# Two expert tables in place of one, a single result row per token, and a re-ordered chunk loop in an RWKV + mixture-of-experts kernel

## The chip, the cores and the metric

The kernel runs on one core of a Trainium2 chip. The metric is the device time of one execution in microseconds (us). Engines: PE is TensorE, ACT is ScalarE, DVE is VectorE, POOL is GpSimd, and SP issues plain DMAs. POOL issues the indirect DMAs, which scatter 128 rows at a time to row numbers held in SBUF.

## The reference, cut to what matters

The first half (time mixing, a log-space recurrence over 2048 tokens of each of 8 sequences) is untouched but for the order of a few steps. The second half is the mixture of experts: each of N = 16384 tokens goes through a shared expert and through its two best of 8 routed ones, and the two kinds of results are added before the last layer norm.

```python
x = x + layernorm(attn(layernorm(x), ...))              # x is (8, 2048, 256)
# ffn on xf = layernorm(x), n = 16384 tokens, d = 256, E = 8, K = 2
probs = softmax(xf @ router_w)
topw, topi = top_k(probs, 2)
combine[n, topi] += topw
h = silu(einsum('nd,edf->nef', xf, w1)); ye = einsum('nef,efd->ned', h, w2)
routed = einsum('ne,ned->nd', combine, ye)
shared = sigmoid(xf @ shared_gate_w) * (silu(gate) * up @ shared_down)
x = x + layernorm(routed + shared)
```

## The kernel before, in words

There are four stages, one after the other.

**The chunk loop** takes the tokens in NCH = 32 chunks of TC = 512. It is a software pipeline: in loop turn i, PE projects chunk i-1 (`proj`), and works on the output product, the router and the shared expert of chunks i-3 to i-5; every engine has its own such list of steps, written out by hand, and the lists are held together by semaphores alone. Each engine does its list in order. Per chunk, DVE picks the two experts (`route`), turns the ranks that PE sums up (`ranks`, bf16 products of the choice masks) into row numbers `ixs` (`place`) and writes the weights behind the token's normed row `h2n` (`weights`). POOL then scatters the row twice, once per choice (`scatter(m, 0)` and `scatter(m, 1)`, four indirect DMAs of 128 rows each), into `d_xd`, which has one region per expert. `h2n` is one buffer, so ACT writes the next chunk's rows (`h2_normed`) only after all eight scatters of the chunk before have landed; POOL computes the scale for it (`scale_h2`) behind those scatters in its own queue. The shared expert's result `ysh`, halved by `weights`, is written by SP to both rows that a token has in `d_y` (lines 402 to 405). During turns 17 to 32, every other turn, ACT and DVE split one expert's weights into a high and a low part (`experts_high`, `experts_low`), one 128x1024 operation each.

**The transition.** After the last chunk, DVE makes the table of blocks (`counted` and the steps behind it: for each block of BLK = 256 rows its expert and its start row), SP writes zero rows behind each expert's last row (`tails`, 8 regions and one more, each with a register load from `tail`), and loads the first blocks.

**The block loop** runs over NB = 2N/BLK + 7 = 135 blocks of 256 rows of one expert. For each, SP loads the rows (`load_block`, four buffers), PE transposes them (`block_in`, 4 instructions), multiplies by w1 (`block_hidden`, 12) and, two blocks later, by w2 (`block_out`, 12); ACT and DVE split each operand into high and low parts; DVE weighs the result into one of six buffers `yb` (`y_out`), and POOL adds it to `d_y` by two indirect DMAs with `compute_op=add` (lines 544 to 548). DVE's `ends` waits for the scatter of eight blocks ago. PE waits at three places for signals that PE itself gives: `s_yp` in `block_in`, `s_Tx` in `block_hidden`, `s_hid` in `block_out`.

**The final stage** goes over the 32 chunks again: SP loads the two rows per token from `d_y` (`y0C`, `y1C`) and x1 (`load_rest`; 12 chunks of it are already loaded in the block loop), DVE adds the two (`total`) and takes the statistics (`stats`), POOL makes the scale (`norm_scale`), ACT applies it, DVE adds x1 (`final`), SP writes the output.

## Time and profile before

| what | value |
|---|---|
| time, median of 3 runs | 1822.88 us (1819.39 to 1824.19) |
| the profiled execution | 1824.77 us |
| span from its first to its last instruction | 1822.6 us |
| PE busy | 1518.0 us (83% of the span) |
| DVE busy | 1466.1 us (80%) |
| ACT busy | 1395.4 us (77%) |
| POOL busy | 1076.9 us (59%) |
| mean granted TensorE clock | 0.928 |

The busy times are means over four stages with different limits, so they are read by stretch: to about 1030 us the chunk loop, to 1134.8 us the transition, to 1658.3 us the block loop and its last scatters, then the final stage. The span and the profiled execution differ by 2.2 us, which lies outside of the first and the last instruction.

### The profile page before, as it was taken

The page shows a single profiled execution, that of the slowest core. Times are in us where ns is not written, and L with a number is a line of the kernel's source. Part 1 is how long each engine was busy: PE and PEld are TensorE (multiplying, and loading weights), DVE is VectorE, ACT ScalarE, POOL GpSimd, SP SyncE. Part 2 cuts the span into 40 slices and gives each one's busy share as a digit, 9 for nine tenths or more (in the row PEclk, how much of TensorE's full clock was granted, in tenths as well). Part 3 has the DMA queues.
Part 4 walks back from the last instruction along what each step waited for, and adds up shares of the span by engine and source line. Part 5 has one row for each costly group of instructions (what it writes and reads, how often), then busy time and mean ns, then how long its engine had stood idle before and what let it go on. Part 6 is the DMA issues. An engine that isn't in the chain of part 4 may idle for free.

```text
span 1822.6 us, 34848 instructions
## 1 busy us (share of the span) xinstructions
PE 1518.0 (83%) x9764; PEld 1346.6 (74%) x9764; DVE 1466.1 (80%) x3533; ACT 1395.4 (77%) x2577; POOL 1076.9 (59%) x985
## 2 busy tenths in 40 slices
PE   4899999999999999999999935999999999980000
PEld 3688888888888888888888835999888888870000
DVE  4799989999998998989999844887777776764888
ACT  3799999999999999999999853776666666652434
POOL 1245546455563654646555351788888888886556
PEclk8999999999999999999999966999999999995555
DMA  6123434343333433334333234998888888877997
GB/s 202 47 84 118 136 115 139 118 144 105 118 119 106 142 106 107 126 99 142 106 116 108 75 128 158 249 181 144 144 145 146 143 146 143 146 114 232 417 417 299
DMA packets 184043, 274.67 MB, mean 151 GB/s; under 512 B 17712, under 2 KB 139568, under 8 KB 183856
## 3 DMA queue, kind: packets, MB, share of 16 engines
q1 hardware_dynamic: 132688, 201.37, 32.8%
q0 software_dynamic: 51168, 71.07, 22.4%
q8 instruction: 84, 1.38, 0.3%
q14 instruction: 103, 0.84, 0.2%
HBM read 127.53 MB, written 144.85 MB: 149 GB/s over the span
## 4 chain that ended last, share of the span: by engine, by line
PE 51%; issue 12%; POOL 10%; DVE 9%; DMA 9%; ACT 2%; DVEq 2%; SPq 1%; POOLq 0%; ACTq 0%
PE PS L1283 39%; POOL d_y L547 7%; PE PS L1275 3%; PE PS L1459 2%; PE PS L1477 2%; POOL d_xd L522 2%; DMA d_y<-nx,ixb 2%; DMA d_y<-x,ixb 2%; PE PS L1346 2%; PE PS L1344 2%; DMA d_y<-xin,ixb 2%; DVE bst L877 1%; DMA rkl<-d_y 1%; DMA al<-d_y 1%; DMA shl<-d_y 1%
## 5 line engine op out<-in xcount | busy, mean ns | idle before, releaser
L522 POOL DMA_INDIRECT d_xd<-h2n,ixs x256 | 319.4, 1248 | 271.6 <-DVE h2n L1056 190.3
L1283 PE MATMUL PS<-hTh,wqh 128*128 128x512 f32 x768 | 307.4, 400 | 16.8 <-ACT kk L581 11.5
L1283 PE MATMUL PS<-hTh,wql 128*128 128x512 f32 x768 | 306.9, 400 | 0.0
L1283 PE MATMUL PS<-hTl,wqh 128*128 128x512 f32 x768 | 306.5, 399 | 0.0
L1283 PEld LDWEIGHTS PS<-hTh,wqh 128*128 128x128 f32 x768 | 146.8, 191 | 53.0 <-ACT kk L581 12.4
L547 POOL DMA_INDIRECT d_y<-xin,ixb x90 | 143.4, 1593 | 52.5 <-DVE xin L1229 28.5
L1283 PEld LDWEIGHTS PS<-hTh,wql 128*128 128x128 f32 x768 | 146.3, 191 | 34.6
L1283 PEld LDWEIGHTS PS<-hTl,wqh 128*128 128x128 f32 x768 | 146.9, 191 | 33.3
L547 POOL DMA_INDIRECT d_y<-nx,ixb x90 | 142.5, 1584 | 27.4 <-issue 21.9
L547 POOL DMA_INDIRECT d_y<-x,ixb x90 | 142.2, 1580 | 27.4 <-issue 19.8
L482 POOL TENSOR_SCALAR var<-mv 128x4 f32<-128x4 f32 x64 | 64.4, 1006 | 154.4 <-DVE mv L882 154.2
L502 POOL TENSOR_SCALAR var<-sq 128x4 f32<-128x4 f32 x32 | 8.7, 272 | 172.4 <-ACT sqo L672 172.4
L1283 PE MATMUL PS<-h2h,wgh 128*128 128x512 f32 x256 | 106.6, 416 | 0.0
L1477 PE MATMUL PS<-weh,h2h 128*128 x360 | 106.1, 295 | 0.0
L1283 PE MATMUL PS<-h2l,wgh 128*128 128x512 f32 x256 | 101.4, 396 | 0.0
L1477 PE MATMUL PS<-weh,h2l 128*128 x360 | 101.2, 281 | 0.0
L1477 PE MATMUL PS<-wel,h2h 128*128 x360 | 101.2, 281 | 0.0
L1283 PE MATMUL PS<-h2h,wgl 128*128 128x512 f32 x256 | 100.9, 394 | 0.0
L1459 PE MATMUL PS<-rkh 128*128 128x256 f32 x268 | 80.4, 300 | 15.9 <-DVE rkl L1239 12.7
L1459 PE MATMUL PS<-hTh,shh 128*128 128x256 f32 x272 | 82.4, 303 | 11.8 <-DVE shl L1239 5.8
L485 POOL TENSOR_TENSOR rstd<-var,mhalf 128x4 f32<-128x4 f32 x64 | 87.0, 1359 | 5.3
L826 ACT ACTIVATE al<-PS 128x512 f32<-128x512 f32 x90 | 53.9, 599 | 44.2 <-PE PS L1459 37.7
(301 smaller groups left out, 5631.8 us busy)
## 6 DMA issues: line engine op xcount, KB each, us to landing
d_y<-ysh SPq DMA_DIRECT2D x64, 512.0 KB
xin<-in_L_attn_x SPq DMA_DIRECT2D x32, 512.0 KB, 3.9
x<-in_L_attn_x SPq DMA_DIRECT2D x32, 512.0 KB, 3.9
d_x<-x SPq DMA_DIRECT2D x32, 512.0 KB
kk<-d_xd SPq DMA_DIRECT2D x34, 272.0 KB
vv<-d_xd SPq DMA_DIRECT2D x34, 272.0 KB
tr<-d_xd SPq DMA_DIRECT2D x34, 272.0 KB
dl<-d_xd SPq DMA_DIRECT2D x33, 272.0 KB
```

What stands on the lines that cost most here:

```text
L482: g.tensor_scalar(var[:, w, :], mvw[:, :, 1], EPS, None, ALU.add).then_inc(s_va[w], 1)
L485: g.tensor_tensor(rstd[:, w, :], var[:, w, :], mhalf[:, :], ALU.pow).then_inc(s_rs[w], 1)
L522: g.indirect_dma_start(d_xd, bass.IndirectOffsetOnAxis(ap=ixs[:, k:k + 1], axis=0), h2n[:, j, :], None).then_inc(s_sct, 16)
L547: g.indirect_dma_start(d_y, bass.IndirectOffsetOnAxis(ap=ixb[:, w % 8, j:j + 1], axis=0), yb[w % NYB][:, j, :], None, compute_op=ALU.add). ...
L826: A.activation(sil[u % 3], hidB[u % 3][:, :], ACT.Silu).then_inc(s_sil, 1)
L877: V.bn_stats(bst[:, k, j, :], tile(j)).then_inc(s_bst[w], 1)
L1275: ins = nc.tensor.transpose(bank[a][:, j * P:(j + 1) * P], src[:, j, a * P:(a + 1) * P], ident[:, :])
L1283: ins = mm_(out_ap, l, r, start=(k == 0), stop=(k == len(todo) - 1))
L1344: mm_(both, h2h[:, a, at], rwp[:, a, :], start=(a == 0), stop=False)
L1346: ins = mm_(both[:, 0:RW], h2l[:, a, at], rwp[:, a, 0:RW], start=False, stop=(a == H - 1))
L1459: ins = mm_(hidB[u % 3][:, f * D:(f + 1) * D], l, r, start=(k == 0), stop=(k == len(todo) - 1))
L1477: ins = mm_(outB[w % 3][:, j * D:(j + 1) * D], l, r, start=(k == 0), stop=(k == len(todo) - 1))
```

## The change

- **Two tables.** The blocks of first choices and those of second choices are kept apart: `d_xd` becomes two tensors, `tb`, `pos`, `cnt`, `tail`, `tabo/x/e/p` get a leading index of 2, and there are NB1 = 64 + 7 = 71 blocks per choice, NB = 142 in all.
- **One row per token.** `d_y` has N rows. The shared result is scattered by POOL (`shared_scatter`, four indirect DMAs per chunk) into `d_xs`, in the order of the first choices. In the first 71 blocks SP loads those rows into `yb` (`load_shared`), DVE adds the routed result to them, and POOL writes them by indirect DMAs without `compute_op`. The other 71 blocks are added with `compute_op=add` as before; POOL starts them when all of the first 71 have landed. The final stage loads one row per token; `total` is gone.
- **Tails.** SP writes 16 of them before the first block (8 of `d_xd[0]`, 8 of `d_xs`), plus three at fixed rows, and the 8 of the second table (`tail_2`) behind the loads of blocks 1 to 8.
- **Order.** The experts' weights are split in the turns NCH+2 and NCH+3 of the loop. `ranks` of the last two chunks is put between the two halves of the gate product. K's, V's, up's and the ranks' PSUM banks are dealt out anew, with another order of `up` and `proj(0)` on PE. `own_exp` moves from the start of a turn to the end of the one before, `weighed` behind `shared`. POOL does `scale_in` last in a turn, with `shared_scatter` behind it.
- **PE's waits for its own signals** in the three block functions are gone.

```diff
-    NB = 2 * N // BLK + E - 1
-    NF = 2 * N // BLK
+    NF = N // BLK
+    NB1 = NF + E - 1
+    NB = 2 * NB1
...
-        pV = [PS[1], PS[5]]
+        pV = [PS[1], PS[0]]
...
-        pU = [PS[4], PS[3]]
+        pU = [PS[0], PS[3]]
...
-        pRT, pRK = PS[0], PS[0]
+        pRT, pRK = PS[0], PS[4]
...
+                for s in range(2):
+                    sp.dma_start(d_xd[s][E * CAP:E * CAP + BLK, :].rearrange("(p j) d -> p j d", p=P), zt
+                                 ).then_inc(s_tail, 16)
+                sp.dma_start(d_xs[E * CAP:E * CAP + BLK, :].rearrange("(p j) d -> p j d", p=P), zt[:, :, 0:D]
+                             ).then_inc(s_tail, 16)
                 sp.wait_ge(s_tab, 1)
                 for e in range(E):
...
+                for e in range(E):
+                    r = sp.value_load(tail[0:1, 0, e:e + 1], min_val=0, max_val=E * CAP - BLK)
+                    sp.dma_start(d_xs[bass.ds(r, BLK), :].rearrange("(p j) d -> p j d", p=P), zt[:, :, 0:D]).then_inc(s_tail, 16)
...
-                if i - 6 == NCH - 1:
-                    tails()
-                if on(i - 6):
-                    sp.wait_ge(s_ys, n(i - 6, NT, NT))
-                    for s in range(2):
-                        sp.dma_start(ys_a[s, i - 6], ysh[:, :, :]).then_inc(s_st2, 16)
...
+            tails()
...
+            sp.wait_ge(s_scy, 16 * NT * NCH)
...
+            def load_shared(b):
+                if b >= NYB:
+                    sp.wait_ge(s_yo[b % NYB], 32 * (b // NYB))
+                r = sp.value_load(tabx[0:1, 0, b:b + 1], min_val=0, max_val=E * CAP)
+                sp.dma_start(yb[b % NYB], d_xs[bass.ds(r, BLK), :].rearrange("(p j) d -> p j d", p=P)
+                             ).then_inc(s_yl[b % NYB], 16)
...
             for b in range(NB):
+                if b == NB1:
+                    sp.wait_ge(s_tail2, 16 * E)
                 load_block(b)
+                if 1 <= b <= E:
+                    tail_2(b - 1)
...
+                if 0 <= b - 2 < NB1:
+                    load_shared(b - 2)
...
+            def shared_scatter(m):
+                pool.wait_ge(s_pl, n(m, NPL, L_IX))
+                for j in range(NT):
+                    pool.wait_ge(s_ys, n(m, NT, j + 1))
+                    g.indirect_dma_start(d_xs, bass.IndirectOffsetOnAxis(ap=ixs[:, m % 2, j:j + 1], axis=0),
+                                         ysh[:, j, :], None).then_inc(s_scy, 16)
...
-            for i in range(NCH + 4):
+            for i in range(NCH + 6):
...
+                if on(i - 4):
+                    scale_o(i - 4)
+                if i - 6 == NCH - 2:
+                    shared_scatter(i - 6)
+                if on(i - 5):
+                    scatter(i - 5, 0)
+                    scatter(i - 5, 1)
+                if on(i - 4):
+                    scale_h2(i - 4)
                 if 0 < i < NCH:
                     scale_in(i)
...
+                if on(i - 6) and i - 6 != NCH - 2:
+                    shared_scatter(i - 6)
...
+                    if w == NB1:
+
+                        for i in range(NYB):
+                            pool.wait_ge(s_yo[i], 32 * ((NB1 - i + NYB - 1) // NYB))
...
+                if i == NCH + 2:
+                    experts_high(EORDER[0:4])
                 if on(i - 4):
                     h2_normed(i - 4)
...
-                if 17 <= i < 17 + 2 * E and i % 2:
-                    experts_high([(i - 17) // 2])
                 if on(i - 3):
                     squares_o(i - 3)
+                if i == NCH + 2:
+                    experts_high(EORDER[4:7])
...
+                if m >= 2:
+
+                    dve.wait_ge(s_sct, 16 * 2 * NT * (m - 1))
+                    dve.wait_ge(s_scy, 16 * NT * (m - 1))
+                V.tensor_copy(ixs[:, m % 2, :], posa[:, :]).then_inc(s_pl, 1)
...
+                if i == NCH + 3:
+                    experts_low(EORDER[3:E])
...
+                    if w < NB1:
+                        V.scalar_tensor_tensor(out=t, in0=part, scalar=cwb[:, w % 8, j:j + 1], in1=t, op0=ALU.mult,
+                                               op1=ALU.add).then_inc(s_y, 1)
...
-            def total(c):
...
+                if NCH - 2 <= i - 4 < NCH:
+
+                    free((i - 4, s_h2l, 2, 2), (i - 2, s_tr, 2, 2), (i - 5, s_pl, NPL, L_TB))
+                    ranks(i - 4)
...
-                    if a and t >= 4:
-                        pe.wait_ge(s_yp, t - 3)
...
-                        if f == 0 and k == 3 and u + 1 < NB:
-
-                            pe.wait_ge(s_Tx, u + 2)
...
-                        if j == 0 and k == 3:
-                            pe.wait_ge(s_hid, min(w + 3, NB))
```

## Rows read from the trace of the kernel before

**Rows 1.** Busy time by stretch: from:to, length, engines, PEclk, DMA share, GB/s
```profile
200.00:400.00 200.00, 200.00 (x1175) 172.58 (x1174) 182.22 (x451) 192.09 (x369) 107.15 (x105) 1.00 0.38 124
1140.00:1658.00 518.00, 467.20 (x3741) 445.40 (x3740) 366.90 (x936) 322.29 (x533) 428.13 (x270) 0.98 0.87 152
1700.00:1750.00 50.00, 0.00 (x0) 0.00 (x0) 39.67 (x97) 20.24 (x40) 27.83 (x40) 0.50 1.03 416
```

**Rows 2.** The same view, a loop turn without and one with an expert's weights
```profile
512.50:544.40 31.90, 31.90 (x189) 27.48 (x188) 28.42 (x67) 30.62 (x59) 16.86 (x16) 1.00 0.34 118
544.40:577.25 32.85, 32.25 (x189) 27.56 (x188) 30.87 (x75) 31.45 (x62) 16.08 (x20) 1.00 0.36 115
```

**Rows 3.** Costliest groups, then POOL's timeline in one turn: start, us, engine, operation
```profile
L522 POOL DMA_INDIRECT d_xd<-h2n,ixs x256 | 319.4, 1248 | 271.6 <-DVE h2n L1056 190.3
...
436.57 1.94 POOL L522 DMA_INDIRECT d_xd<-h2n,ixs  x1 [0.30 <-issue]
...
441.35 0.96 POOL L522 DMA_INDIRECT d_xd<-h2n,ixs  x1 [0.30 <-issue]
...
450.62 0.26 POOL L487 TENSOR_TENSOR nb<-nmx,rstd 128x4 f32<-128x4 f32 x1
```

**Rows 4.** Timeline of DVE in the turn before: row numbers, then weights
```profile
428.40 0.17 DVE L1033 CAST ixs<-posa 128x8 uint32<-128x8 f32 x1
...
429.35 0.19 DVE L1047 TENSOR_REDUCE ssum<-pw 128x4 f32<-128x32 f32 x1 [0.37 <-ACT pw L721]
```

**Rows 5.** Timeline of ACT: an expert's high part, and the last chunks' normed rows
```profile
712.58 1.04 ACT L574 CAST weh<-wel 128x1024 fp32r<-128x1024 f32 x1
...
1060.17 1.04 ACT L739 CAST rkh<-ee 128x1024 fp32r<-128x1024 f32 x1 [2.91 <-DVE ee L1068]
1061.38 2.08 ACT L657 ACTIVATE h2n<-x,nb,rstd 128x256 f32<-128x256 f32 x4 [0.16 <-POOL nb L514]
```

**Rows 6.** Timeline of DVE, POOL and SP in the transition
```profile
1106.36 0.19 DVE L1020 TENSOR_TENSOR pos<-PS,tb 128x32 f32<-128x32 f32 x1 [3.90 <-PE PS L1366]
...
1109.39 1.07 POOL L522 DMA_INDIRECT d_xd<-h2n,ixs  x1 [18.49 <-DVE h2n L1056]
...
1119.51 1.07 POOL L522 DMA_INDIRECT d_xd<-h2n,ixs  x1 [0.30 <-issue]
...
1114.31 10.15 SPq L375 DMA_DIRECT2D d_xd<-vv  x8
...
1128.27 0.37 SPq L422 DMA_DIRECT2D kk<-d_xd  x1
```

**Rows 7.** Chain that ended last, its ends of the block stage: start, us, what
```profile
1134.81 2.91 PE PS L1459 x12
...
1628.18 1.62 PE PS L1459 x12
...
1654.51 3.75 DMA d_y<-x,ixb
```

**Rows 8.** Groups of 1200 to 1600 us (busy, mean ns), then timelines of POOL and PE
```profile
L547 POOL DMA_INDIRECT d_y<-x,ixb x72 | 114.1, 1585 | 21.9 <-issue 15.8 <-DVE x L1229 3.1 <-DVE ixb L1221 2.7
...
1146.01 1.70 POOL L547 DMA_INDIRECT d_y<-xin,ixb  x1 [25.43 <-DVE xin L1229]
...
1184.63 0.66 PE L1437 MATMUL PS<-ident,kk 128*128 128x128 f32 x4
...
1188.02 0.66 PE L1437 MATMUL PS<-ident,vv 128*128 128x128 f32 x4
```

**Rows 9.** Timeline of DVE and POOL in the final stage
```profile
1673.71 1.22 DVE L1254 TENSOR_TENSOR ysh<-h2h,rkl 128x1024 f32<-128x1024 f32 x1
...
1677.88 1.22 DVE L1254 TENSOR_TENSOR h2n<-h2l,shh 128x1024 f32<-128x1024 f32 x1
...
1741.36 1.31 POOL L482 TENSOR_SCALAR var<-mv 128x4 f32<-128x4 f32 x1 [2.02 <-DVE mv L882]
...
1744.18 0.21 POOL L487 TENSOR_TENSOR nb<-nmn,rstd 128x4 f32<-128x4 f32 x1
```

More of the change, by code:

```diff
@@ L52, in rwkv_moe @@
     out_c = out.rearrange("b (c p j) d -> (b c) p (j d)", j=NT, p=P)
-    d_xd = nc.dram_tensor("d_xd", [E * CAP + BLK, XW], F32).ap()
-    NSINK = E + NB - NF + 1
-    d_y = nc.dram_tensor("d_y", [2 * N + 1 + NSINK * BLK, D], F32).ap()
-    ys_a = d_y[1:2 * N + 1, :].rearrange("(s c j p) d -> s c p j d", s=2, j=NT, p=P)
+    d_xd = [nc.dram_tensor(f"d_xd{s}", [E * CAP + BLK, XW], F32).ap() for s in range(2)]
+    d_xs = nc.dram_tensor("d_xs", [E * CAP + BLK, D], F32).ap()
+    NSINK = E + NB1 - NF + 1
+    d_y = nc.dram_tensor("d_y", [N + 1 + NSINK * BLK, D], F32).ap()
     with ExitStack() as ctx:
@@ L275, in rwkv_moe @@
         s_yo = [sem(f"s_yo{i}") for i in range(6)]
+        s_yl = [sem(f"s_yl{i}") for i in range(6)]
         s_Tx = sem("s_Tx")
@@ L286, in rwkv_moe @@
         s_y = sem("s_y")
-        s_cx = [sem(f"s_cx{i}") for i in range(12)]
-        s_cy2 = [sem(f"s_cy2{i}") for i in range(6)]
-        s_sum = sem("s_sum")
+        s_cx = [sem(f"s_cx{i}") for i in range(14)]
         s_nrm = sem("s_nrm")
@@ L297, in rwkv_moe @@
         NRO = 7
[L299 to L300 removed]
+        L_POS, L_TB, L_PM, L_POSA, L_IX, L_DST = range(1, 7)
+        NPL = 6
         W_SUM, W_CWT, W_SG, W_CW = range(2, 6)
@@ L386, in _ @@
             sp.dma_start(x1[:, :, :], x_v[0]).then_inc(s_xr, 16)
-            for i in range(NCH + 6):
+            for i in range(NCH + 4):
                 if i % 2 == 0 and i // 2 < E:
@@ L545, in _ @@
                 pool.wait_ge(s_y, 2 * (w + 1))
-                for j in range(2):
-                    g.indirect_dma_start(d_y, bass.IndirectOffsetOnAxis(ap=ixb[:, w % 8, j:j + 1], axis=0),
-                                         yb[w % NYB][:, j, :], None, compute_op=ALU.add).then_inc(s_yo[w % NYB], 16)
+                if w < NB1:
+                    for j in range(2):
+                        g.indirect_dma_start(d_y, bass.IndirectOffsetOnAxis(ap=ixb[:, w % 8, j:j + 1], axis=0),
+                                             yb[w % NYB][:, j, :], None).then_inc(s_yo[w % NYB], 16)
+                else:
+                    if w == NB1:
+                        for i in range(NYB):
+                            pool.wait_ge(s_yo[i], 32 * ((NB1 - i + NYB - 1) // NYB))
+                    for j in range(2):
+                        g.indirect_dma_start(d_y, bass.IndirectOffsetOnAxis(ap=ixb[:, w % 8, j:j + 1], axis=0),
+                                             yb[w % NYB][:, j, :], None, compute_op=ALU.add).then_inc(s_yo[w % NYB], 16)
             for c in range(NCH):
@@ L1152, in _ @@
                 if on(i - 3):
+                    weighed(i - 3)
                     sums(i - 3)
@@ L1202, in _ @@
             step(11)
+            both = [P, 2, NBP]
+            V.tensor_tensor(tbf[:, 1, :, :], tbf[:, 1, :, :], iot2[:, :].unsqueeze(1).to_broadcast(both), ALU.add
+                            ).then_inc(s_tb, 1)
+            step(12)
             V.tensor_scalar(iot2[:, :], iot2[:, :], -(NF - 1.0) * BLK, None, ALU.add).then_inc(s_tb, 1)
-            step(12)
-            V.scalar_tensor_tensor(out=tabo[:, :], in0=tbf[:, 0, :], scalar=E - 0.5, in1=iot2[:, :], op0=ALU.is_ge,
-                                   op1=ALU.mult).then_inc(s_tab, 1)
```

252 lines of the change are left out of this document (126 added, 126 removed).

## The prediction

> **What bounds the kernel now.** I read busy time by stretch first. In the chunk loop PE is busy 200.00 of 200 us at full clock, with ACT at 192 and DVE at 182; in the block stage PE is at 90% and POOL at 83%, and the DMA share is 0.87; in the final stage the DMA share is 1.03 at 416 GB/s and no engine is near full [rows 1]. The timelines then tell what the block stage hangs on. One `compute_op=add` scatter holds POOL for 1.585 us, plus 0.30 us between two, so a block's two take 3.77 us [rows 8], while PE, where nothing holds it, starts a block every 3.39 us (transposes at 1184.63 and 1188.02) [rows 8]. And PE's last product starts at 1628.18 while POOL's last scatter starts at 1654.51, 26 us later [rows 7]: POOL bounds the block stage. So there are four limits: PE, then a latency chain in the transition, then POOL, then DMA bytes.
>
> **Chunk loop.** A turn takes 31.90 us without an expert's weights and 32.85 with them [rows 2]; ACT has only 1.3 us to spare in the first kind, and the cast takes 1.04 of it [rows 5]. Eight such turns become plain: 8 x 0.95 = **-8 us**. PE's own work per turn is unchanged (`ranks` is wider, still 11 tiny products), and the new order and banks put no wait where an operand is late in the trace, so I cost them at nothing; so also `own_exp`, `weighed` and the one operation fewer in `place`. That cover is PE's: DVE and ACT have a turn's rest of 3.5 and 1.3 us [rows 2].
>
> What is added is `shared_scatter`, four indirect DMAs on POOL per chunk. The kind's mean is 1.248 us, the least 0.96, and 1.94 where DVE's scans run beside it [rows 3]; with 0.30 between, four take 6.2 us, or 5.0 to 9.0. They stand behind `scale_in`, which ends at 450.88 [rows 3], so they end at 457.1, and land 2.2 us later (the last block scatter took 3.75 us from its start to its landing, 1.55 of it on POOL [rows 7, 8]): 459.3. Who waits? `place` of the next chunk must not write `ixs` before: that cast is due at 428.40 + 31.9 = 460.3, and behind it on DVE stand `weights` and the residual, for which POOL's next scatters and PE wait [rows 4]. The wait is covered by 1.0 us, and `weights` itself has 0.37 us more, since it waits for ACT [rows 4]. I take nothing, and keep 0 to 1.8 us per turn for the range: 1.8 is what four scatters of 1.94 give (450.9 + 9.0 + 2.2 = 462.1 against 460.3).
>
> How long a scatter takes beside DVE decides this. The row shows 1.94 us against 0.96 for the same instruction [rows 3]. The Trainium skill (GPSIMD Engine Reference, Key points) says that GpSimd shares its SBUF interfaces with VectorE and contends with instructions "in a 2-port perf mode or with two SBUF inputs"; by that rule the new scatters, beside DVE's subtractions from PSUM with one SBUF input, would mostly run in 0.96, and if all four were blocked the sum would be that of the slower rival below.
>
> **Transition**, two chains. (a) ACT casts four experts before `h2_normed` of chunk 30. In the trace that starts at 1061.38, right behind the cast that ends at 1061.21 [rows 5], so four casts of some 0.97 us each come on the path: +3.7. Three more stand before the exponentials of chunk 30, for which `weights` had 0.85 us of cover in `place`: about +1.8, since the earlier `ranks` gains nothing there. So chunk 31's routing comes 5.5 us later. The five low parts on DVE and ACT's last cast fall in DVE's idle time after 1081. For chunk 31 `ranks` comes 3.7 us earlier (DVE waited 3.90 us for it [rows 6]), so the table is only 2 us later. (b) POOL's last eight scatters took from 1109.39 to 1120.58 [rows 6]. Now chunk 30's shared scatters stand before them and wait for its down product (+5.5, to about 1120.6), then eight (11.2) and four (5.1): 1137, and 2.2 to land, 1139.1, before SP may load block 0. SP's chain is shorter: the tails cost 1.27 us each (10.15 for 8) [rows 6], 16 of them 20.3, from about 1110: 1130.4, landed 2.5 later. So the first load moves from 1128.27 [rows 6] to about 1139.5, 11 later. I take **+10**, 4 to 16: the lower end has POOL's part overlap better, the upper has contended scatters and longer table steps.
>
> **Block stage**, from PE's first product at 1134.81 to the last landing at 1658.26: 523.5 us [rows 7]. After: the first scatter comes 11.2 us in [rows 7, 8]. A first-choice block takes POOL only 2 x (0.96 + 0.30) = 2.5 us, if a plain block scatter costs what a plain row scatter does [rows 3], so PE bounds those: 3.39 less what the dropped waits cost, under 0.1, for they stand behind three products or transposes already issued: 3.35. 70 x 3.35 = 234.5. Then 2.5 for the last, 2.2 to land, as POOL waits for all; PE runs on meanwhile. Then 142 x (1.585 + 0.30) = 267.7, and 1.9 for the landing: 11.2 + 234.5 + 2.5 + 2.2 + 267.7 + 1.9 = 520.0, **-3**. The seven blocks more thus eat what the cheap scatters give. Range -9 (1.85 per scatter as in its uncontended form) to +11 (blocks at 3.55: loads of shared rows and x1 together). DVE adds from SBUF in `y_out` instead of only weighing, beside PE; its share is 71% [rows 1].
>
> **Final stage**, 1822.6 - 1658.3 = 164.3 us. Bytes before: 33.6 MB of `d_y`, 10.5 of x1 (20 chunks), 16.8 out: 60.8 MB, at 416 GB/s 146 us, so 18 lie at the ends. After: 16.8 + 9.4 + 16.8 = 43.0 MB, 103 us; with the same ends 121. What is late next: DVE's chunk takes 1677.88 - 1673.71 = 4.17 us where data is there; without `total` (1.22 and a gap of 0.04) 2.91, 93 us for 32. POOL's takes 1741.36 to 1744.39, 3.03, and some 0.15 between [rows 9]: 102, about as much as the bytes. So I take 121, **-43**, with 112 to 132 (POOL at 3.6 per chunk if it contends).
>
> The Trainium skill (DMA: Bandwidth & Descriptors, Where 436 GB/s comes from) gives about 358 GB/s as the HBM limit of a core; by that figure the stage would take 120 + 18 = 138 and the gain be 26. The trace shows 416 over 50 us [rows 1], so the measurement decides.
>
> **Sum**, against the profiled execution's span: 1822.6 - 8 + 10 - 3 - 43 = 1778.6. That execution took 1824.77, 1.9 above the median, so the same 44 off the median gives 1822.88 - 44 = **1779**.
>
> **Rivals.** *A, plain scatters are no cheaper in the block loop.* Then POOL bounds both halves: 142 x 1.885 = 267.7 instead of 234.5 (and 1.2 more for the last), +34 minus the little that PE's slack gives: 1811. For it: the two kinds differ in source buffer and row length, not only in the addition. Against: 1.55 never goes below in 270 scatters, 0.96 is the usual of 256.
> *B, the place where the shared scatters stand is too tight.* 0.5 to 1.2 us per turn, in 31 turns: +15 to +37, 1794 to 1816. For it: cover of 1.0 us only. Against: the mean scatter fits.
> *C, slower than before.* The same wait, when every one of the four shared scatters runs at the doubled 1.94 us: 1.8 us per turn x 31 = 56, 1835. It decides from 1.45 us per turn (44/31), that is from a shared scatter of 1.84 us on average. Against it: 0.96 is usual where DVE does not scan, and after 451 it does not.
> *D, the edges are kinder:* transition +4, block stage -9, final stage -52 (bytes alone, shorter ends): 1822.88 - 65 = 1758 at the far end.
>
> **How the numbers follow.** Forecast 0.70 (1766 to 1794); A 0.08; B 0.12; C 0.03; D beyond 1765 0.07. The range leaves out C, most of A and of D: 1763 to 1802. A measurement of this kernel tells 0.3%, some 5.5 us, from no change. Faster by more: everything but C and the end of B, 0.95; within: 0.02; slower: 0.03.
>
> **What would show it.** Right: turns 17 to 32 of 31.9 us; POOL's scatters of 0.96 us and PE's blocks of 3.35 in the first half of the block loop, 3.77 in the second, with a POOL backlog only in the second; a final stage of 121 us with DMA still near 1.0. Wrong: a wait of DVE before `ixs` in every turn (B, C); 1.55 us for plain block scatters (A); a final stage paced by POOL at 3.6 us per chunk; first load later than 1145, above all if POOL's scatters were not last there but SP's tails.

## The result, and the profile after

The changed kernel took **1779.08 us** (median of 4, 1778.62 to 1782.03) against 1822.88 before: ratio 0.9766, interval 0.9749 to 0.9783. Its profiled execution has a span of 1776.9 us, 45.7 under before's 1822.6. That is the predicted time. It is not the whole result: run again later, the same kernel took 1816.29 at the same mean granted clock (0.936, against 0.937; run `c1_after_again` below), and most of the experiments went into why.

First the stages of the profiled execution, each end read from a timeline (PE's last product of chunk 31's projections, PE's first product of the blocks, the last landing, the end):

```
stage                        before   after    change   predicted
projections of chunk 31 end  1030.70  1019.11   -11.6      -8
transition                    104.11   113.45    +9.3     +10
block stage                    523.5    522.0    -1.4      -3
final stage                    164.3    122.3   -42.0     -43
```

Busy time by stretch, kernel after, to be laid beside [rows 1]; the block stage is split where the adding scatters begin:

```profile
200.00:400.00 200.00, 200.00 (x1183) 172.93 (x1183) 182.23 (x432) 192.55 (x367) 132.75 (x130) 1.00 0.33 111
1140.00:1380.00 240.00, 235.52 (x2007) 233.86 (x2006) 203.09 (x503) 172.46 (x288) 156.00 (x141) 1.00 0.86 274
1385.00:1654.00 269.00, 226.20 (x1882) 219.95 (x1880) 183.15 (x469) 160.03 (x264) 224.46 (x142) 0.96 0.85 136
1633.00:1654.00 21.00, 0.00 (x0) 0.00 (x0) 0.53 (x2) 0.00 (x0) 16.48 (x11) 0.51 0.63 74
1700.00:1750.00 50.00, 0.00 (x0) 0.00 (x0) 39.85 (x125) 28.23 (x55) 33.81 (x55) 0.50 1.00 393
```

In the loop PE is still full and POOL has gone from 107 to 133 us in 200. In the first half of the blocks PE is at 98% and POOL at 65%; in the second POOL, not PE, sets the pace. The final stage still has the DMA engines full.

The `PEclk` column is 1.00 in the first two rows. The 0.96 of the third is its end alone: PE's last product ends at 1630.3, the granted clock goes to half at 1633.3 and stays there (fourth row, 0.51), and from 1385 to 1633 it is 1.00. So the clock costs the blocks nothing here.

The loop's new scatters, in POOL's timeline, and behind them DVE's cast that must wait for them (compare [rows 3] and [rows 4]):

```profile
480.56 1.08 POOL L553 DMA_INDIRECT d_xs<-ysh,ixs  x1 [0.47 <-issue]
...
484.66 0.96 POOL L553 DMA_INDIRECT d_xs<-ysh,ixs  x1 [0.30 <-issue]
...
489.71 0.17 DVE L1086 CAST ixs<-posa 128x8 uint32<-128x8 f32 x1
```

```profile
DVE ixs L1086 <- DMA d_xs<-ysh,ixs: 2.5, 6, 0.6
```

```profile
L553 POOL DMA_INDIRECT d_xs<-ysh,ixs x76: 956/1023/1227, 321.6 to 898.4; - x76
...
DMA to landing us min/median/max: 2.4/3.6/5.3
```

The second fence is DVE's list of waits in 300 to 900 us (total, times, longest): the shared scatters made the cast wait six times, 2.5 us in all. The third has their durations in the same stretch (ns, shortest, median, longest) and the time from the start of one to its landing. Their place is wide enough, but only just: in the 25 turns from 160 to 940 us the last rows of a chunk land 2.4 to 4.4 us after POOL's scatter ends (median 3.0), and the cast follows that landing by 1.0 us in the median, in seven turns at once. No turn is longer for it.

The transition, timelines of ACT, POOL and SP, then SP's waits in 1095 to 1135 us (compare [rows 5] and [rows 6]):

```profile
1046.94 3.88 ACT L618 CAST weh<-wel 128x1024 fp32r<-128x1024 f32 x4
1050.72 2.07 ACT L701 ACTIVATE h2n<-x,nb,rstd 128x256 f32<-128x256 f32 x4
...
1107.12 1.79 POOL L546 DMA_INDIRECT d_xd<-h2n,ixs  x1 [0.31 <-issue]
...
1118.97 0.96 POOL L553 DMA_INDIRECT d_xs<-ysh,ixs  x1 [0.30 <-issue]
...
1122.77 0.96 POOL L553 DMA_INDIRECT d_xs<-ysh,ixs  x1 [0.31 <-issue]
...
1107.67 10.78 SPq L385 DMA_DIRECT2D d_xs<-ee  x8
1126.11 0.38 SPq L432 DMA_DIRECT2D kk<-d_xd  x1
```

```profile
SPq L422 <- DMA d_xs<-ysh,ixs: 6.7, 1, 6.7
```

Four casts stand before `h2_normed`; POOL's row of twelve scatters ends at 1123.73, after SP's tails at 1118.45; and SP then waits for the last shared rows before it loads a block that doesn't need them.

The blocks, timelines of PE and POOL and the end of the chain (compare [rows 7] and [rows 8]):

```profile
1246.07 0.60 PE L1499 MATMUL PS<-ident,tr 128*128 128x128 f32 x4
1249.31 0.60 PE L1499 MATMUL PS<-ident,dl 128*128 128x128 f32 x4
...
1380.21 1.26 POOL L583 DMA_INDIRECT d_y<-nx,ixb  x1 [0.30 <-issue]
1385.08 1.61 POOL L591 DMA_INDIRECT d_y<-x,ixb  x1 [3.60 <-DVE xin L1295]
...
1650.98 3.58 DMA d_y<-xin,ixb
```

```profile
L583 POOL DMA_INDIRECT d_y<-nx,ixb x48 | 54.0, 1125 | 26.7 <-DVE nx L1292 16.1 <-issue 10.6
...
L591 POOL DMA_INDIRECT d_y<-xin,ixb x48 | 75.9, 1582 | 14.6 <-issue 11.9 <-DVE ixb L1279 1.8 <-DVE xin L1295 0.6
```

A first-choice block starts every 3.26 us on average (3.24 to 3.28 by turns) instead of 3.40; a plain scatter holds POOL for 1.1 us, an adding one for 1.58; between the halves POOL stands 3.60 us; from 1385.08 to 1650.98 lie 141 scatters of 1.886 each.

### The profile page after: what moved, and what is told of

It is laid out like the page before. It is cut to its first block, busy times and chain, and to the rows that moved or that the text cites. A ratio compares the mean times of both kernels' runs of the same rounds, so it can differ in the third digit from the quotient of the medians.

```text
span 1776.9 us, 36129 instructions
## 1 busy us (share of the span) xinstructions
PE 1512.4 (85%) x9960; PEld 1359.6 (77%) x9960; DVE 1451.5 (82%) x3518; ACT 1408.8 (79%) x2605; POOL 1149.0 (65%) x1127
## 3 DMA queue, kind: packets, MB, share of 16 engines
q8 instruction: 86, 1.41, 0.3%
## 4 chain that ended last, share of the span: by engine, by line
PE 65%; POOL 8%; DMA 7%; issue 7%; DVE 4%; ACT 3%; SPq 2%; DVEq 1%; POOLq 0%; ACTq 0%
PE PS L1341 46%; PE PS L1518 6%; PE PS L1534 5%; POOL d_y L591 5%; PE PS L1333 3%; PE PS L1499 2%; DMA d_y<-x,ixb 2%; PE PS L1404 2%; DMA d_y<-nx,ixb 2%; PE PS L1402 1%; POOL d_xd L546 1%; DMA d_y<-xin,ixb 1%; DVE bst L925 1%; DMA dl<-d_y 1%; POOL var L506 1%
## 5 line engine op out<-in xcount | busy, mean ns | idle before, releaser
L546 POOL DMA_INDIRECT d_xd<-h2n,ixs x256 | 317.8, 1241 | 234.5 <-DVE h2n L1108 164.1
L1341 PE MATMUL PS<-hTh,wqh 128*128 128x512 f32 x768 | 306.1, 399 | 16.3 <-ACT kk L625 10.6
L553 POOL DMA_INDIRECT d_xs<-ysh,ixs x128 | 134.8, 1053 | 58.8 <-issue 45.3
L1341 PEld LDWEIGHTS PS<-hTl,wqh 128*128 128x128 f32 x768 | 146.1, 190 | 33.1
L1534 PE MATMUL PS<-weh,h2l 128*128 x380 | 106.2, 279 | 0.0
L1534 PE MATMUL PS<-wel,h2h 128*128 x380 | 106.1, 279 | 0.0
L1518 PE MATMUL PS<-rkh 128*128 128x256 f32 x284 | 86.4, 304 | 12.1 <-DVE rkl L1304 10.6
L509 POOL TENSOR_TENSOR rstd<-var,mhalf 128x4 f32<-128x4 f32 x64 | 92.9, 1451 | 5.3
L1518 PE MATMUL PS<-hTh,shh 128*128 128x256 f32 x284 | 86.5, 305 | 7.8 <-DVE shl L1304 7.8
L865 ACT CAST hTh<-PS 128x512 fp32r<-128x512 f32 x71 | 41.7, 587 | 60.2 <-PE PS L1499 60.2
L591 POOL DMA_INDIRECT d_y<-x,ixb x48 | 75.5, 1573 | 17.9 <-issue 10.7
L591 POOL DMA_INDIRECT d_y<-xin,ixb x48 | 75.9, 1582 | 14.6 <-issue 11.9
L583 POOL DMA_INDIRECT d_y<-xin,ixb x48 | 52.5, 1093 | 48.1 <-DVE xin L1292 40.2
```

The source lines that it names most:

```text
L509: g.tensor_tensor(rstd[:, w, :], var[:, w, :], mhalf[:, :], ALU.pow).then_inc(s_rs[w], 1)
L546: g.indirect_dma_start(d_xd[s], bass.IndirectOffsetOnAxis(ap=ixs[:, m % 2, k:k + 1], axis=0), h2n[:, j, :], None).then_inc(s_sct, 16)
L553: g.indirect_dma_start(d_xs, bass.IndirectOffsetOnAxis(ap=ixs[:, m % 2, j:j + 1], axis=0), ysh[:, j, :], None).then_inc(s_scy, 16)
L583: g.indirect_dma_start(d_y, bass.IndirectOffsetOnAxis(ap=ixb[:, w % 8, j:j + 1], axis=0), yb[w % NYB][:, j, :], None).then_inc(s_yo[w % NY ...
L591: g.indirect_dma_start(d_y, bass.IndirectOffsetOnAxis(ap=ixb[:, w % 8, j:j + 1], axis=0), yb[w % NYB][:, j, :], None, compute_op=ALU.add). ...
L865: copy(xTh[t % 2], PS[t % 2][:, :]).then_inc(s_xh, 1)
```

## The experiments

Twelve kernels ran, in four series; each was timed beside the kernel before, whose medians were 1821.24, 1822.45, 1821.41 and 1822.10 us. The spans and stretches below are of each kernel's profiled execution.

### PE's waits for its own signals

`e1_before_no_own_waits` (series 1), before without them:

```diff
-                    if a and t >= 4:
-                        pe.wait_ge(s_yp, t - 3)
...
-                            pe.wait_ge(s_Tx, u + 2)
...
-                            pe.wait_ge(s_hid, min(w + 3, NB))
```

> The kernel before with PE's three waits for its own signals taken out of the blocks, nothing else. My theory: all 135 blocks of before end at the pace of POOL's adding scatters (2 x 1.885 us a block against some 3.4 us of PE), so the time stays, 0 us, within 1; PE's busy time in a block may fall by 0.13 us without anybody asking for it. Rival: the waits hold up the chain of every block, and the time falls by 135 x 0.13 = 18 us.

Measured: 1822.65 us, ratio 1.0005 (0.9989 to 1.0022). The theory holds. While POOL has not yet fallen behind, PE runs full in both kernels, and the waits can be read off: same stretch 1145 to 1210 us, first the kernel before, then this one:

```profile
1145.00:1210.00 65.00, 65.00 (x536) 63.27 (x535) 55.58 (x135) 46.27 (x78) 53.93 (x34) 1.00 1.00 247
```

```profile
1145.00:1210.00 65.00, 65.00 (x560) 65.00 (x559) 53.62 (x134) 48.13 (x80) 54.73 (x34) 1.00 1.00 250
```

560 products instead of 536 in the same 65 us, or 3.26 us a block instead of 3.40: **0.14 us a block**. The loads of weights (PEld) are at 63.27 with the waits and at 65.00 without: the little gap is there. POOL's adds take it all back.

`e2_after_own_waits` (series 1), after with them:

```diff
+                    if a and t >= 4:
+                        pe.wait_ge(s_yp, t - 3)
...
+                            pe.wait_ge(s_Tx, u + 2)
...
+                            pe.wait_ge(s_hid, min(w + 3, NB))
```

> The kernel after with PE's three waits for its own signals put back in both halves of the blocks. My theory: the first 71 blocks are PE-bound now, their pace goes from 3.27 us back to 3.40 us, and the time rises by 71 x 0.13 = 9 us (against after's 1779.1: 1788); the second half, bound by the adding scatters at 2 x 1.886 us a block, doesn't change. Rival, the value of the prediction: the waits cost under 0.04 us a block, the faster pace has another reason (XW rows, the table loads, the shorter scatter), and the time rises by 3 us or less.

Measured: 1831.63 us, 1.0053 (1.0036 to 1.0070): 53 above after's first measurement, where the theory said 9. In the second half PE's blocks take 3.40 us while it catches up, as expected (1441.92 to 1516.90, 22 of them). In the first half they take 4.1. PE's waits in 1150 to 1430 us, and one of them with DVE's and POOL's timeline:

```profile
PE PS L1501 <- PE PS L1540: 28.8, 41, 0.9
```

```profile
1214.25 0.96 POOL L583 DMA_INDIRECT d_y<-nx,ixb  x1 [0.30 <-issue]
...
1215.84 0.88 DVE L1292 SCALAR_TENSOR_TENSOR x<-PS,cwb,x 128x256 f32<-128x256 f32 x2 [0.31 <-PE PS L1540]
...
1215.86 0.44 PE L1501 MATMUL PS<-ident,vv 128*128 128x128 f32 x2 [0.87 <-PE PS L1540]
```

PE waits for a product that it issued last at 1214.48 and that takes 0.28 us; DVE waits for the same signal and is let go at the same moment, 0.63 us after POOL's scatter ends at 1215.21. So here PE's signal came about a microsecond late, for both (the end of a product is modelled in the trace, so a product that itself ended late would look the same). In the second half that wait shows no idle time at all. This fitted neither theory; what follows came out of the next two runs and the control.

### Late signals

`e5_shared_wait_later` (series 1) moves one wait of SP:

```diff
-            sp.wait_ge(s_scy, 16 * NT * NCH)
...
             def load_shared(b):
+                if b == 0:
+                    sp.wait_ge(s_scy, 16 * NT * NCH)
```

> The kernel after with SP's wait for the last shared scatters moved from ahead of the first block's load to ahead of the first load of shared rows. My theory: SP waited 6.7 us there for the last of chunk 31's shared rows to land (about 1125.2), while the scatter of its hidden rows had ended at 1118.7 and the tails at 1118.5; the first load starts at about 1121.5 instead of 1126.1, and the time falls by 4 to 5 us (1774 to 1775). Rival: the first blocks are held by SP's own register loads in blocks 1 to 13, an earlier start is eaten up there because the shared rows are then late for the first y, and the time falls by 1 us or less.

Measured: the first load comes 103.1 us after chunk 31's projections instead of 107.0, and the first block product 109.5 after them instead of 113.5, so the 4 us are there. But the time is 1799.48, 0.9873 (0.9847 to 0.9898): the plain scatters last to 1412.9 instead of 1380.2. The run with the experts, below, showed the same, and so I took a control.

`c1_after_again` (series 2) is the kernel after, unchanged.

> The kernel after, unchanged, as a control beside the others of this series. The run with the experts back in the loop and the run with the later wait for the shared rows both ended 33 us later than after's trace, and both lost it in the first 71 blocks (last plain scatter at about 1412 instead of 1380), in stalls of ACT and PE of 3 to 4 us each whose releaser the trace doesn't know. Theory A: those stalls belong to the chip of that series and not to the edits, and after itself takes 1795 to 1810 here, with the same stalls in the same stretch. Theory B: the edits brought them about, and after stays at 1779, within 3.

Measured: **1816.29 us, 0.9962 (0.9948 to 0.9976)**. Theory A holds in that the edits are innocent; that it is a matter of the chip fell later, in series 3. Chunk loop, transition, second half and final stage are within 3 us of after's; the first half of the blocks lasts from 1147.3 to 1422.0, 274.7 us instead of 235.7. Two falls of the granted clock to half, 3.4 us each, are some 3 of those 39 us. In the lists, `remote` is a releaser that the trace can't name. First the stretch, then ACT's waits in 1200 to 1380 us, and last ACT, PE and POOL around one wait:

```profile
1140.00:1420.00 280.00, 250.15 (x2028) 241.20 (x2027) 196.34 (x504) 166.08 (x291) 143.38 (x140) 0.99 0.76 238
```

```profile
ACT al L873 <- PE PS L1518: 18.4, 12, 3.9
ACT rkh L865 <- remote: 13.2, 7, 1.9
ACT hTh L865 <- remote: 12.4, 7, 2.6
```

```profile
1182.89 0.28 PE L1518 MATMUL PS<-hTh,shl 128*128 128x256 f32 x1
1183.73 1.01 POOL L583 DMA_INDIRECT d_y<-xin,ixb  x1 [0.47 <-issue]
...
1184.78 0.36 PE L1518 MATMUL PS<-rkh 128*128 128x256 f32 x1
...
1185.05 0.96 POOL L583 DMA_INDIRECT d_y<-xin,ixb  x1 [0.30 <-issue]
...
1186.88 0.60 ACT L873 ACTIVATE al<-PS 128x512 f32<-128x512 f32 x1 [3.85 <-PE PS L1518]
```

ACT needs the hidden product that ends at 1183.17. It starts at 1186.88; PE has meanwhile done an output product and the next block's hidden one (to 1186.45). POOL's last scatter of a row ends at 1186.01, 0.87 us before. In after's first trace ACT's longest such wait in that stretch is 0.2 us:

```profile
ACT al L873 <- PE PS L1518: 2.0, 11, 0.2
```

Late signals aren't confined to the blocks. In the chunk loop, which has plain scatters too, DVE waits for the router's product; its waits in 200 to 1000 us of this kernel:

```profile
DVE lg L1045 <- remote: 44.3, 21, 2.3
```

Such waits, up to 2.2 or 2.3 us each, stand in the loops of all changed kernels of series 1, 2 and 4; after's first trace and series 3 have none. They cost little there: a turn takes up to 32.1 us instead of 31.83, and the loop ends 2.7 us later.

The table takes, for all kernels, every start of this step of ACT (`A.activation(sil...)`) after an idle time over 0.25 us, and how long after the end of its own block's hidden product it came (a start within 2 us of the last plain scatter counts with the plain ones):

```
stretch                                       starts   longest   over 1 us
adding scatters: before                         58      0.10         0
  e1                                            65      0.04         0
  second half of all others but e4             302      0.08         0
plain scatters:  after (first), e8, e11          6      0.04         0
  e10                                            3      0.04         0
  c1, first half                                37      3.84        10
  e3, e5, e6, e7, first half                   156      4.99        43
  e4, first and second half                     85      4.97        27
  e12, paused part / rest                    13 / 19  3.77/4.93   3 / 4
  e2, first half                                 4      0.16         0
```

In e2's first half it is PE and DVE that show the late signal, as seen above. Of the 87 starts over 1 us late, 57 come 0.6 to 1.2 us after the end of a scatter of POOL. That points to how POOL issues them; this part is argued from the times alone. An engine that stands for want of its next instructions would look alike, and the trace speaks against it: fetches of instructions are among its DMA packets, in 60 of the 87 waits none ends inside the wait, and in 5 one ends in the last 0.5 us before the start.

`e4_second_plain` (series 2) makes the second half's scatters plain:

```diff
-                                             yb[w % NYB][:, j, :], None, compute_op=ALU.add).then_inc(s_yo[w % NYB], 16)
+                                             yb[w % NYB][:, j, :], None).then_inc(s_yo[w % NYB], 16)
```

> The kernel after with the adding scatters of the second half of the blocks made plain ones (the results of second choices replace those of first choices, their addition is left out). My theory: the kind of the scatter sets its price, not the row or the source: 1.0 to 1.1 us of POOL each instead of 1.89 a scatter, so that the second half becomes PE-bound like the first, 71 x 3.27 = 232 us instead of 268, and the time falls by 34 to 37 us. Rival: the price is that of rows that are already there or of the number of rows under way, and the scatters stay at 1.5 us and more: the time falls by 15 us or less.

Measured: 1805.74 us, 0.9898 (0.9867 to 0.9929). The kind sets the price: the second half's scatters hold POOL for 1.0 us instead of 1.57, with the same rows and source. The gain was not to be had: the half lasts from 1407.0 to 1675.7, 268.7 us, against 264.8 in `c1_after_again`. (The total is 10.6 us below c1's, but the first half, which the edit doesn't touch, is 19 us shorter: late signals come and go from one execution to the next.) Second half of c1, then of this kernel, and this kernel's waits of ACT in 1430 to 1660 us:

```profile
1430.00:1690.00 260.00, 222.19 (x1846) 215.76 (x1844) 180.18 (x461) 156.90 (x259) 217.61 (x140) 0.97 0.84 138
```

```profile
1410.00:1670.00 260.00, 230.16 (x1870) 221.11 (x1868) 180.02 (x466) 149.81 (x263) 134.82 (x135) 0.99 0.46 137
```

```profile
ACT al L873 <- remote: 22.8, 8, 4.9
ACT rkh L865 <- remote: 17.8, 9, 2.7
ACT hTh L865 <- remote: 15.6, 6, 2.6
```

One word of the code, on one chip, in one series, turned a half without late signals into one full of them; and the DMA share there is 0.46 instead of 0.84, so full DMA engines are not the cause. What else the word changes is the pace: the half is no longer held up by POOL. And POOL's being busy is not it either: in c1's second half POOL issues without a rest, and every signal is in time.

`e10_pause` and `e11_two_waits` (series 3) were meant as cures:

```diff
+                        if j == 0:
+                            if w:
+                                pool.wait_ge(s_pad, w)
+                            g.memset(hTh[:, 1, 0:TC].bitcast(F32), 0.0).then_inc(s_pad, 1)
```

```diff
+                            pe.wait_ge(s_Tx, u + 2)
...
+                            pe.wait_ge(s_hid, min(w + 3, NB))
```

> The kernel after with a fill of 128x512 on POOL (some 0.5 us) between the two plain scatters of each of the first 71 blocks. In the runs of after on the two other chips ACT waits up to 3.9 us for a product of PE that is long done, whenever POOL issues plain scatters one behind the other, and it is released 0.3 to 1.1 us after POOL's row of two or four ends. Theory: POOL's plain scatter holds back PE's signals, and a gap of 0.8 us in place of 0.3 lets them through; the waits over 1.7 us go, the first 71 blocks take 235 to 245 us instead of 270 to 275 (first to last plain scatter), and the time falls by 25 to 35 us against the run of after with the same stalls (1816). Rival: the signals are held by the rows under way in the DMA engines, or by PE's own running ahead, and the pause changes nothing, or costs up to 71 x 0.5 = 36 us more.

> The kernel after with two of PE's three waits for its own signals put back (for the transposes within the hidden product, for the hidden product within the output product), the one for the output product within the transposes left out. Theory: of the 54 us that the three waits cost in the first 71 blocks nearly all was the third, which asks for a product that PE has only just issued; the two others ask for work that lies 1.4 us back and cost under 0.13 us a block, but they keep PE from running ahead, so that ACT's long waits stay away: first 71 blocks about 240 us. Rival: the signals are late whoever waits for them, so the two waits only add to it and the first 71 blocks take 275 us or more.

Measured: 1784.59 us, 0.9793 (0.9770 to 0.9816), and 1783.91, 0.9794 (0.9776 to 0.9813); one wait of ACT over 1.7 us in the first half of each. That looked like two cures, but `e8_extra_4` of the same series, with after's block stage, had three such waits, after itself two, and c1 had 32; by the table nothing was late in that series, so neither run tests its theory. It is the chip on which e3 and e5 had late signals in series 1: a condition that comes and goes, and not a property of one chip. What e11 does give is the size of the two waits: 3.34 us a block against 3.26.

`e12_both_half_paused` (series 4) has the pause in 36 of the 71 blocks only, and both edits of SP (e5 and e6):

```diff
+                        if j == 0 and w < 36:
```

> The kernel after with both edits of SP together (the wait for the last shared scatters ahead of the first load of shared rows; the second table's tail writes in blocks 16 to 30 and the x rows' loads in blocks 34 to 47), and with the fill on POOL between the two plain scatters in blocks 0 to 35 only; blocks 36 to 70 have none, as in after. It is its own control: the last run with after's block stage (the one with extra shared scatters) did not show ACT's long waits on a chip on which two runs of an hour before had shown them, so the pause of all blocks proved nothing. If the waits are about and the pause lets the signals through, blocks 0 to 35 run at 3.27 us and blocks 36 to 70 at 3.7 to 4.0, in all about 1790. If the waits are about and the pause is no help, both parts run at 3.7 to 4.0: 1800 or more. If they are not about, both parts run at 3.27, the first product of the blocks starts at about 1129 instead of 1132.6 (4 us), PE doesn't wait for the loads of the first 20 blocks (4 to 5 us), and the time is 1769 to 1773, 6 to 10 us below after's 1779.1. Rival for that case: one of the two gains is eaten by POOL, whose second half starts only when its scatters have landed: 1775 or more.

Measured: 1807.48 us, 0.9901 (0.9873 to 0.9930). Signals were late, so it tests the pause. The part with the pause, then the part without:

```profile
1143.00:1270.00 127.00, 117.65 (x981) 114.65 (x981) 100.01 (x245) 81.12 (x140) 88.67 (x105) 1.00 0.82 262
1272.00:1400.00 128.00, 112.20 (x921) 108.04 (x921) 89.28 (x229) 74.77 (x132) 67.41 (x67) 1.00 0.74 238
```

By POOL's first scatters of blocks 0, 36 and 70 (1142.55, 1273.54, 1406.20) a block takes 3.64 us with it and 3.90 without, and there are 7 waits of ACT over 1.7 us against 16. Neither of the outcomes that I had written down. The first ten blocks, before anything was late, lie in the paused part; from block 10 on it takes 3.75, so the pause takes away a quarter to two fifths of the loss against 3.26 at best, and signals up to 3.77 us late stand inside it. It is no cure.

### Parts of the sum

`e3_experts_in_loop` (series 1) puts the experts' split back into turns 17 to 32, for ACT as shown and for DVE likewise:

```diff
-                if i == NCH + 2:
-                    experts_high(EORDER[0:4])
...
+                if 17 <= i < 17 + 2 * E and i % 2:
+                    experts_high([(i - 17) // 2])
```

> The kernel after with the split of the experts' weights into high and low parts put back into turns 17 to 32 of the chunk loop, as in before. My theory: each of the seven turns between two expert turns costs 1.1 us again, the loop ends 7.5 to 9 us later (projections of chunk 31 from 1019.1 to about 1027), and the stretch from there to the first product of the blocks shrinks by 3 to 5 us, because ACT's eight casts (3.88 + 2.94 + 0.97 us) no longer stand before h2_normed and the exponentials; in sum +3 to +6 us (1782 to 1785). Rival: the casts in the transition are covered, nothing is given back there, and the time rises by 8 us or more (1787). Second rival: they cost there what they cost in the loop, 0 us.

Measured: 1802.24 us, 0.9884 (0.9854 to 0.9913), with late signals in the blocks, so the time says little and the stages are compared. Chunk 31's projections end at 1031.25, against 1020.09 and 1019.65 in the two other changed kernels of the series: +11.4. The turn between two `nx` transposes of PE is 31.83 us where it has no weight, and 32.8 to 33.1 with one, but 36.11 and 34.40 in two of the seven. The first of the two:

```profile
605.89:642.00 36.11, 35.38 (x189) 30.05 (x188) 31.63 (x73) 32.23 (x62) 23.52 (x24) 0.91 0.28 90
```

The granted clock was at half for 6.8 us there and for 3.4 us in the other (0.95 over the turn); these falls make 4.3 of the 11.4. PE had stood for 0.73 and 0.60 us a little before, as it does in the other turns with a weight and not in the plain ones. Of the 21 turns with a weight in before, e1 and this kernel three have such a fall; of after's turns in that stretch, none. Transition 106.03 instead of 113.5: 7.4 back. I had expected 7.5 to 9 and 3 to 5. So what the loop gains by moving the experts, 7.1 us without the falls of the clock, is paid again in the transition, 7.4; what is left is the falls, where they happen.

`e8_extra_4` (series 3) issues the shared scatters of chunks 0 to 29 twice:

```diff
+                    if m < NCH - 2 and j < 4:
+                        g.indirect_dma_start(d_xz, bass.IndirectOffsetOnAxis(ap=ixs[:, m % 2, j:j + 1], axis=0),
+                                             ysh[:, j, :], None).then_inc(s_scy, 16)
```

> The kernel after with each of the four shared scatters of chunks 0 to 29 issued a second time, into rows that nobody reads: 4 x 1.04 us more of POOL in a turn of the chunk loop. The block stage is that of after, so it is also the control of this series. Theory, from the places in POOL's queue: what stands behind the shared scatters is due 2.0 to 2.7 us later than it comes, so 1.5 to 2.2 us of the 4.2 show in each of some 28 turns and the projections of chunk 31 end 42 to 60 us later than 1020. Rival: POOL has 31.8 - 21.4 = 10 us of idle time in a turn and all of it is cover, 0 us.

Measured: 1841.31 us, 1.0113 (1.0088 to 1.0137); projections end at 1079.20, +59 in 30 turns, 1.97 each (1.9 in the usual turn; in three turns of 37.5 to 38.2 us the granted clock also fell to half for 3.4 us). DVE's waits in 300 to 900 us, then POOL's last and DVE's cast in one turn:

```profile
DVE ixs L1093 <- DMA d_xs<-ysh,ixs: 71.6, 18, 6.1
```

```profile
504.00 1.08 POOL L558 DMA_INDIRECT d_xz<-ysh,ixs  x1 [0.46 <-issue]
...
513.28 0.96 POOL L560 DMA_INDIRECT d_xs<-ysh,ixs  x1 [0.30 <-issue]
...
515.79 0.17 DVE L1093 CAST ixs<-posa 128x8 uint32<-128x8 f32 x1 [3.43 <-DMA d_xs<-ysh,ixs]
```

The wait is where rival B and C had put it. The row of eight takes 10.24 us where four took 5.06: 5.2 more (my 4.2 had left out the 0.30 between two), of which 1.97 show, so 3.2 us were cover. The cast follows POOL's end by 1.55 us here, where it comes later in the turn; in after it stood 4.09 us behind it, so the landing had 2.5 us to spare before the cast and DVE gave 0.7 more. In after's own turns, though, the rows landed later, at 2.4 to 4.4 us, and the room was 1.0 us in the median. POOL's 10 us of idle time in a turn are of no use; the place in its queue is.

`e6_tails_spread` (series 2):

```diff
-                if 1 <= b <= E:
-                    tail_2(b - 1)
+                if 16 <= b < 16 + 2 * E and b % 2 == 0:
+                    tail_2((b - 16) // 2)
...
-                if b >= 8 and b - 8 < NS:
-                    load_rest(b - 8)
+                if b >= 34 and b - 34 < NS:
+                    load_rest(b - 34)
```

> The kernel after with the second table's eight tail writes moved from blocks 1 to 8 to every other block from 16 to 30, and the first 14 loads of x rows from blocks 8 to 21 to blocks 34 to 47. My theory: PE's waits for block loads at 1155 to 1187 (5 to 6 us in all) come from SP, which pays three register loads of some 1.2 us a block there; with two a block it keeps up with 3.27 us, and the time falls by 4 to 5 us against the control. Rival: the loads themselves are late because the DMA engines are full there (their share is 1.01 in 1160 to 1200), and the time falls by 1 us or less.

Measured: 1818.99 us, 0.9969 (0.9949 to 0.9988), no different from c1. In 1138 to 1215 us PE waits for loads 0 times, against 4.0 us in c1 and 4.4 in after's first trace. One of c1's:

```profile
1166.08 0.96 PE L1499 MATMUL PS<-ident,vv 128*128 128x128 f32 x4 [3.25 <-DMA vv<-d_xd]
```

Theory and rival aren't separated by this: in 1160 to 1200 us the edit also lowers the DMA share, from 0.94 to 0.71. What speaks for the theory is SP's own timeline in after: from 1130 to 1156 us it issues with hardly a rest, and the loads of blocks come 3.5 to 4.3 us apart, where PE asks for one every 3.26. That the late signals ate the gain is the likely reading and not shown. In e12, which has both edits, the first product comes 109.9 us after the projections and PE runs nine blocks at 3.26 before anything is late; both gains are there as pieces, their sum in a time without late signals was not measured.

`e7_no_x_loads` (series 2):

```diff
-                    if m + NS < NCH:
-                        load_rest(m + NS)
```

> The kernel after without the 18 loads of x rows in the final stage (9.4 MB of 43.0; the sums of chunks 14 to 31 use the rows of an earlier chunk, so that part of the result is left out). My theory, as in the prediction: the final stage is bound by bytes, and falls by 9.4 MB at 416 GB/s = 23 us, from 122 to about 100, where DVE's 2.9 us a chunk (93) begins to bound it. Rival: the stage goes by the latency of its chain (load, statistics, POOL, ACT, sum, store) at 3.8 us a chunk, and falls by under 8 us.

Measured: 1797.33 us, 0.9855 (0.9827 to 0.9882). From the last landing the stage takes 107.5 us, against 122.3 in c1: -14.7 for 9.4 MB. Two stretches of this kernel:

```profile
1692.00:1737.00 45.00, 0.00 (x0) 0.00 (x0) 39.57 (x133) 27.24 (x53) 33.90 (x57) 0.50 0.89 322
1737.00:1770.00 33.00, 0.00 (x0) 0.00 (x0) 30.34 (x95) 22.49 (x44) 26.71 (x43) 0.50 0.94 337
```

DVE is at 88 to 92% here, 80% in after. The stage is bound by bytes in after, but only 15 us above the next bound, DVE's 91 us of work and its ends. Between theory and rival.

## Why the prediction was right, and where it was not

**The time.** 1779.08 against 1779, and each stage within 4 us. The hit to 0.1 us is luck twice over. The loop's 3.6 us of extra gain stand against 1.9 us less in the later stages, and the spans differ by 45.7 us where the medians differ by 43.8. And that execution fell in a time in which PE's signals came promptly. In series 2 the same kernel gained 0.4% instead of 2.3%, and neither the forecast nor a rival names this: I took for granted that a stage costs what its instructions cost.

**Chunk loop**, -8 predicted, -11.6 measured. The experts' term was right in size: seven turns, not eight, were 0.95 to 1.41 us above the plain ones in before, 7.6 in all. Mis-sized is "I cost them at nothing" for the new order: 31.91 to 31.83 us in every plain turn, some 2 us. Another 1.7 came before 161 us, nearly all in the first turn (34.85 to 33.34), and is no effect of the change: e1, with before's loop, has 32.28 there, and e11, with after's, 34.93.

**The shared scatters' place.** "Covered by 1.0 us": measured 1.0 in the median, by two errors that cancel: four scatters took 5.06 us, not 6.2, and their landing came 3.0 us behind POOL's end in the median, not 2.2. When POOL is later, the landing is quicker (1.55 us in e8), and the cover is 3.2 in all. B and C had the right mechanism: the wait came when e8 asked for it, and its 1.9 us a turn are near C's 1.8. C's threshold should read 1.42 us a turn (44/31), not 1.45.

**Transition**, +10 and +9.3. Both chains are in the trace as predicted: four casts, 3.88 us together, before `h2_normed`, POOL's row last, not SP's tails. e3 gives 7.4 of the 9.3 to the experts, where I had 5.5, so their move, forecast to gain 2.5 us net, gained nothing but the falls of the clock that the loop is spared. A part that I had not priced on its own is SP's wait for the shared rows ahead of a load that doesn't need them: 4.0 us (e5).

**Block stage**, -3 and -1.4, term by term: first scatter 11.9 us in (11.2 predicted), 234.4 to the last first-choice block (234.5), 6.2 to the first adding scatter (4.7), 267.8 (267.7), 1.7 (1.9). The exact 234.4 hides two errors: the waits are worth 0.14 us a block (e1), not 0.04, which brings 3.26 instead of 3.35, 6 us over 70 blocks; and PE lost 4.4 us to late loads in the first blocks (e6) and some more in catching up. Plain scatters at 1.1 us against 1.58 dispose of rival A; e4 shows that the addition alone makes the difference.

**Final stage**, -43 and -42: bytes moved at 363 GB/s (1660 to 1700 us) and 393 (1700 to 1750) and not at 416, and the ends were shorter. The Trainium skill's 358 GB/s (DMA: Bandwidth & Descriptors, Where 436 GB/s comes from) would have given, as an estimate, 138 us; the stage took 122.3, and 393 over 50 us is again above that figure.

**POOL beside DVE.** By the Trainium skill's rule (GPSIMD Engine Reference, Key points), that GpSimd contends with DVE's instructions in a 2-port mode or with two SBUF inputs, the new scatters should mostly run uncontended, as the prediction read it: the 76 of them in 300 to 900 us have a median of 1.02 us and a longest of 1.23, against 0.96 at least; the trace agrees.

## What to carry to other kernels

Ask of every step that is moved which place it gets in its engine's queue and what is due behind it: 10 us of idle POOL in a turn held 3.2 us of cover. Ask also whether the time that a move saves is paid again where the work goes (here 7.1 us against 7.4). Where a change swaps one kind of DMA for another, let the same kernel run again at another time before believing the gain: here 44 us became 6. And when a run is to say what an edit is worth, compare stages of the traces, not totals.

## What the runs showed of the hardware that I had not expected

- With plain indirect scatters on POOL, signals of PE can reach other engines 1 to 5 us late (87 starts of ACT), and DVE and PE itself by about 1 (e2); two thirds of ACT's late starts come 0.6 to 1.2 us after a scatter of POOL ends. With adding scatters none of 302 starts was over 0.08 us late. The late signals were there in three of the four series here, on three chips, in the chunk loop as in the blocks, and absent in after's first measurement and in series 3, on one of the same chips; what brings them about is **open**. That POOL's issuing holds the signals is the likeliest reading, but a pause of 0.54 us took only a part of the waits away, and nothing here looks into the signal's path.
- PE's three waits for its own signals cost 0.14 us a block as long as signals are in time (e1), two of them 0.08 (e11); with late signals the one in `block_in`, which asks for the product just issued, showed 28.8 us in 41 waits (e2).
- `compute_op=add` costs POOL 0.5 to 0.6 us for each 128 rows over a plain scatter (1.58 against 1.11 in after, 1.57 against 1.00 from c1 to e4, with the same rows and source).
- A load on SP whose address comes from a register costs some 1.15 us of SP (1126.11 to 1127.26 in after), so three a block (3.5 us) are more than a block of 3.26 allows.
- The same four scatters land 2.4 to 4.4 us after POOL's end in after's loop and 1.55 us after it where they come 5 us later in the turn (e8).
